# A recurrent layer's folds, operand copies and state store, shared out anew between ScalarE, VectorE and GpSimd

## The reference

```python
xw = jnp.einsum('ntd,dh->nth', x, Wx) + b
def step(prev_h, xw_t):
    next_h = jnp.tanh(prev_h @ Wh + xw_t)
    return (next_h, next_h)
_, hs = jax.lax.scan(step, h0, jnp.swapaxes(xw, 0, 1))
```

## Time and profile before

| | us |
|---|---|
| median of three runs | 7361.7 |
| profiled execution, its own time | 7363.88 |
| its span, first to last instruction | 7362.1 |
| of it the 128 steps of the recurrent layer, about | 3980 |

### The profile page before, as it was taken

How to read it: one execution, slowest core, us unless ns; L and a number is a source line. 1 busy time by engine, 2 the same in 40 slices (tenths; PEclk the granted TensorE clock), 3 DMA queues, 4 the chain that set the end, 5 groups by cost and what they waited for, 6 DMA issues and landing times. The chain is left out here.

```text
span 7362.1 us, 151269 instructions
## 1 busy us (share of the span) xinstructions
PE 5760.5 (78%) x49639; PEld 3129.6 (43%) x49913; DVE 5820.5 (79%) x11267; ACT 4421.0 (60%) x9397; POOL 2712.0 (37%) x2033
## 2 busy tenths in 40 slices
PE   5877787787778777877787707888888887943989
PEld 3555454455445555544454402333333333531543
DVE  4888988898889888988898669999999995455333
ACT  6877877787778777877787604444444442323322
POOL 2222222222222222222222108999999992000000
PEclk9999999999999999999999859999999998976989
DMA  0000000000000000000000010000000000000000
GB/s 7 2 2 2 2 2 2 2 2 2 2 2 2 2 2 2 2 2 2 2 2 2 10 34 5 4 4 4 4 4 4 4 4 3 0 10 3 0 17 6
DMA packets 14180, 30.30 MB, mean 4 GB/s; under 512 B 3665, under 2 KB 11602, under 8 KB 12434
## 3 DMA queue, kind: packets, MB, share of 16 engines
q1 hardware_dynamic: 13586, 22.47, 1.1%
HBM read 15.12 MB, written 7.34 MB: 3 GB/s over the span
## 5 line engine op out<-in xcount | busy, mean ns | idle before, releaser
L421 ACT ACTIVATE rx_junk<-rx_z 128x384 bf16<-128x384 f32 x2178 | 1371.9, 638 | 0.3
L1005 POOL TENSOR_TENSOR hc<-hh,cg 128x512 f32<-128x512 f32 x1024 | 1277.0, 1267 | 80.4 <-DVE hh L987 75.0
L927 ACT ACTIVATE ps_m<-ps_m,aneg 128x508 f32<-128x508 f32 x1024 | 673.6, 658 | 946.0 <-DVE hh L987 828.7
L987 DVE TENSOR_TENSOR_SCAN hh<-ps_m,bx 128x512 f32<-128x512 f32 x1024 | 1214.0, 1209 | 13.8 <-POOL bx L1009 13.8
L506 POOL TENSOR_TENSOR rx_z<-rx_z 128x512 f32<-128x512 f32 x256 | 384.9, 1504 | 2204.6 <-ACT rh_z L437 2201.5
L891 PE MATMUL ps_m<-hc,pick 128*128 128x512 f32 x2048 | 1056.3, 599 | 9.8 <-POOL hc L1005 8.5
L641 DVE TENSOR_REDUCE rh_ends<-rh_z 128x4 f32<-128x1536 f32 x512 | 960.3, 1919 | 131.0 <-ACT rh_z L437 131.0
L337 PE MATMUL r_ps<-rx_z,negid 128*128 128x256 f32 x2192 | 565.7, 405 | 280.2 <-POOL xsl L549 189.3
L512 POOL TENSOR_TENSOR rx_z<-rx_z 128x1024 f32<-128x1024 f32 x274 | 656.5, 2396 | 73.4 <-DVE rx_z L607 36.7
L313 PE MATMUL r_ps<-rh_z,negid 128*128 128x256 f32 x2048 | 496.8, 384 | 166.2 <-ACT r_ps L432 163.6
L337 PEld LDWEIGHTS r_ps<-rx_z,negid 128*128 128x128 f32 x2192 | 422.8, 202 | 391.0 <-issue 326.6
(11 more groups left out here) (397 smaller groups left out, 10726.0 us busy)
## 6 DMA issues: line engine op xcount, KB each, us to landing
rows_scratch<-pc SPq DMA_DIRECT2D x48, 128.0 KB
rows<-rows_scratch SPq DMA_DIRECT2D x128, 48.0 KB
ew<-in_e SPq DMA_DIRECT2D x3, 1024.0 KB, 7.0
rh_z<-in_x_dn SPq DMA_DIRECT2D x1, 1024.0 KB, 4.8
xcur<-in_x_dn SPq DMA_DIRECT2D x1, 1024.0 KB
out_x<-xcur SPq DMA_DIRECT2D x1, 1024.0 KB, 3.9
qi<-in_f_q SPq DMA_DIRECT2D x1, 384.0 KB, 2.9
xpw<-in_xp_t SPq DMA_DIRECT2D x1, 257.0 KB
```

What stands on the lines that cost most here:

```text
L421: e.activation(junk[:, n % JUNK], xz[i][:, :, n, 2:K2].rearrange("p c k -> p k c"), ACT.Copy, accum_out=xsum[:, i, n:n + 1]).then_inc(x_fo ...
L927: e.activation(da[un % NDA][:, :, 1:T], ps[:, un % 2, :].rearrange("p (n t) -> p n t", n=NG4)[:, :, 1:T], ACT.Exp, scale=aneg[:, 0:1]).the ...
L987: e.tensor_tensor_scan(hh[un % NBUF][:], da[un % NDA].rearrange("p n t -> p (n t)"), bx[un % NBUF][:], 0.0, ALU.mult, ALU.add).then_inc(sc ...
L1005: e.tensor_tensor(hc[un % NHC][:], hh[un % NBUF][:], cg[:], ALU.mult).then_inc(weighted, 1)
```

## The change

ScalarE folds the last two of the 16 sequences of the h chain (`TAIL = 2`), each with an ACTIVATE that accumulates into `ends`, behind its own last `rest` copy; VectorE's fourth reduction covers two sequences in place of four, and `pre` waits for `tail` as well. The four operand copies of the tanh move from ScalarE to GpSimd, as additions of zero or a subtraction from zero with two inputs each, behind the step's second `x_negdifference` and ahead of `x_bias`. The store of h moves from ScalarE to GpSimd, an addition of zero, behind `x_bias`; it waits for h itself, and the loads of `xsp` and `xsl` (s = 6 and 7) come after it in GpSimd's list. VectorE waits for the store of the step before (`kept`) ahead of the tanh.

```diff
@@ ScalarE, in a step
                     for c in range(2, NRC):
                         rest(c)
+                    e.wait_ge(ra, KA * t + A_REST[NRC - 1])
+                    for i_ in range(TAIL):
+                        n = N - TAIL + i_
+                        e.activation(rjunk[:, i_], hz[:, :, n, 2:K2].rearrange("p c k -> p k c"), ACT.Copy,
+                                     accum_out=ends[:, n:n + 1]).then_inc(tail, 1)
                     x_fold(g - 1, other, SECOND, THIRD)
-                    e.wait_ge(v, KV * t + V0 + VSQUARE)
-                    for lo, hi_ in ((1, 6), (7, 9)):
-                        e.activation(t0[:].rearrange("p (n j) c -> p n j c", j=GROUPS * GL)[:, :, lo:hi_, 0],
-                                     x2[:].unsqueeze(2).to_broadcast([128, N, hi_ - lo]), ACT.Copy).then_inc(tri, 1)
-                    e.wait_ge(v, KV * t + V0 + VGUESS)
...
-                    e.activation(entry(2), guess, ACT.Copy, scale=-1.0).then_inc(tri, 1)
-                    e.activation(entry(1), guess, ACT.Copy).then_inc(tri, 1)
                     x_fold(g - 1, other, THIRD, N)
...
-                    e.wait_ge(v, KV * t + V0 + KV)
-                    e.activation(hs[:, bass.ds(t, 1), :], h[:].unsqueeze(1), ACT.Copy).then_inc(ra, 1)
@@ GpSimd, in a step, behind the even sums and differences
+                    e.wait_ge(v, KV * t + V0 + VSQUARE)
+                    for lo, hi_ in ((1, 6), (7, 9)):
+                        wide = lambda x: x.unsqueeze(2).to_broadcast([128, N, hi_ - lo])
+                        e.tensor_tensor(t0[:].rearrange("p (n j) c -> p n j c", j=GROUPS * GL)[:, :, lo:hi_, 0],
+                                        wide(x2[:]), wide(nought[:]), ALU.add).then_inc(tri, 1)
+                    e.wait_ge(v, KV * t + V0 + VGUESS)
...
+                    e.tensor_tensor(entry(1), guess, none, ALU.add).then_inc(tri, 1)
+                    e.tensor_tensor(entry(2), none, guess, ALU.subtract).then_inc(tri, 1)
                     if s == 0:
                         e.wait_ge(xt_mm, i + 1)
                     x_bias(g - 1, s % 2, s)
+                    e.wait_ge(v, KV * t + V0 + KV)
+                    e.tensor_tensor(hs[:, bass.ds(t, 1), :], h[:].unsqueeze(1), nought[:].unsqueeze(1), ALU.add).then_inc(kept, 1)
                     if s == UN - 2:
                         e.wait_ge(xp_mm, UN * i + 2 * UN)
@@ VectorE, in a step
                     for c in range(NRC):
                         e.wait_ge(ra, KA * t + A_REST[c])
-                        j = tl.inc(e.tensor_reduce(ends[:, quarter(c)], fold(hz, quarter(c)), mybir.AxisListType.XY, ALU.add))
+                        n = slice(quarter(c).start, min(quarter(c).stop, N - TAIL))
+                        j = tl.inc(e.tensor_reduce(ends[:, n], fold(hz, n), mybir.AxisListType.XY, ALU.add))
                     tl.wait(j)
+                    e.wait_ge(tail, TAIL * t + TAIL)
...
                     j = tl.inc(e.tensor_tensor(pre[:], ends[:], xwT[:, s, :], ALU.add))
+                    e.wait_ge(kept, t + 1)
```

More of the change, by code:

```diff
@@ L79, in rnn @@
         ends = sb("rh_ends", [128, N])
+        TAIL = 2
+        rjunk = sb("rh_junk", [128, TAIL, D, 3], BF16)
         junk = sb("rx_junk", [128, JUNK, D, 3], BF16)
@@ L110, in rnn @@
             "x_copied", "x_summed", "x_evened", "x_negdiff", "x_rest", "x_folded", "x_biased"))
-        xt_mm, xw_cp, stp, stl, tri = (sem(x) for x in ("xt_mm", "xw_cp", "stp", "stl", "tri"))
+        xt_mm, xw_cp, stp, stl, kept, tri, tail = (sem(x) for x in ("xt_mm", "xw_cp", "stp", "stl", "kept", "tri", "tail"))
         KD = 8
@@ L117, in rnn @@
         A_REST = (7, 8, 11, 12)
-        KA = 13
+        KA = 12
         V_EVEN = (2, 5)
@@ L474, in _ @@
                         rest(c)
-                    x_fold(g - 1, other, SECOND, THIRD)
-                    e.wait_ge(v, KV * t + V0 + VSQUARE)
-                    for lo, hi_ in ((1, 6), (7, 9)):
-                        e.activation(t0[:].rearrange("p (n j) c -> p n j c", j=GROUPS * GL)[:, :, lo:hi_, 0],
-                                     x2[:].unsqueeze(2).to_broadcast([128, N, hi_ - lo]), ACT.Copy).then_inc(tri, 1)
-                    e.wait_ge(v, KV * t + V0 + VGUESS)
-                    guess = gs[:, 1:NS + 1].rearrange("p (ng j) -> p ng j", j=GL + 1)[:, :, 1:]
-                    entry = lambda c: t1[:, :, c].rearrange("p (ng j) -> p ng j", j=GL)
-                    e.activation(entry(2), guess, ACT.Copy, scale=-1.0).then_inc(tri, 1)
-                    e.activation(entry(1), guess, ACT.Copy).then_inc(tri, 1)
+                    e.wait_ge(ra, KA * t + A_REST[NRC - 1])
[3 more added lines that the diff above has]
+                                     accum_out=ends[:, n:n + 1]).then_inc(tail, 1)
+                    x_fold(g - 1, other, SECOND, THIRD)
                     x_fold(g - 1, other, THIRD, N)
@@ L492, in _ @@
                     x_fold(g, at, 0, FIRST)
-                    e.wait_ge(v, KV * t + V0 + KV)
-                    e.activation(hs[:, bass.ds(t, 1), :], h[:].unsqueeze(1), ACT.Copy).then_inc(ra, 1)
         @blk.gpsimd
         def _(e):
+            e.memset(gate[:, 2:3], 0.0).then_inc(kept, 1)
             e.memset(ident[:], 0.0).then_inc(setup, 1)
@@ L538, in _ @@
                         x_negdifference(g, (s + 1) % 2, c)
+                    e.wait_ge(v, KV * t + V0 + VSQUARE)
[4 more added lines that the diff above has]
+                    e.wait_ge(v, KV * t + V0 + VGUESS)
+                    guess = gs[:, 1:NS + 1].rearrange("p (ng j) -> p ng j", j=GL + 1)[:, :, 1:]
+                    entry = lambda c: t1[:, :, c].rearrange("p (ng j) -> p ng j", j=GL)
+                    none = nought[:, 0:1].unsqueeze(2).to_broadcast([128, N * GROUPS, GL])
+                    e.tensor_tensor(entry(1), guess, none, ALU.add).then_inc(tri, 1)
+                    e.tensor_tensor(entry(2), none, guess, ALU.subtract).then_inc(tri, 1)
                     if s == 0:
```

## The result

The changed kernel takes 7549.99 us in the median (7547.47 to 7551.38) against 7359.88 before: 1.0257 times as long, 95% interval 1.0239 to 1.0275, that is 190 us slower. Forecast were 7578 and a range of 7492 to 7690. The profiled execution took 7551.38, its span 7549.6; lines have moved by up to 12, so instructions are named by what they do.

A forecast was written before the change was run, and what follows sets the result against it. The x chain was taken to set the inner step, with the h chain some 0.2 us to spare. From the profiled 7363.9, 48 (inner steps) + 101 (step 6) + 67 (step 7) gave 7580, so 7578 against the median; range 7492 to 7690.

The forecast's parts named there:

- What bounds: Inner steps, ahead of `h_product`: the x chain sets the step; the h chain has some 0.2 us to spare.
- The fourth reduction: VectorE's reduction ahead of `pre`: halving saves between 0 and 0.94 us, but gain taken is 0.
- ScalarE's cover: Ahead of `x_rest_copy`: net some +0.7 us of work against 0.71 idle, taken as 0, bound ±0.2 per inner step.
- The copies and X: GpSimd's copies lengthen the tanh on the h chain by X = 0.75 us; inner steps grow by 0.5, +48 us.
- Step 6: Late `xsp` load +3.57, later h 0.75, slow clock 2.0: together 6.3 us in each of 16 blocks, +101 us.
- Step 7: Load of `xsl` delays `x_remainder`: +3.46 plus 0.75 for later h, 4.2 us in each of 16 blocks, +67 us.
- Copies in the gaps: Rival: GpSimd's copies find gaps in the tanh, inner steps stay at +0; 7507 us, chance 0.18.
- Whole-instruction exclusion: Rival: VectorE stands still throughout GpSimd's copies, 1.59 us with no time given back; 7688 us, chance 0.13.
- The loads not felt: Rival: TensorE's waits in steps 6 and 7 are covered by something else; between 7362 and 7426 us, chance 0.05.
- The h chain as bound with the saving getting through: Rival: h comes up to 0.96 us earlier in every step through `pre`; 7339 us, chance 0.02.

The follow-up runs named there:

- The folds alone: Kernel before with only ScalarE's two folds and the halved fourth reduction; copies and store stay on ScalarE: 7444.10 us, ratio 1.0114.
- halved warm matmuls: Kernel before with five warm matmuls in a step in place of ten: 7328.79 us, ratio 0.9955.
- the warm matmuls ahead of the wait: Changed kernel; in step 6 alone the ten warm matmuls stand ahead of TensorE's wait for `xsp`, not behind `product`: 7521.15 us, ratio 1.0222.
- the store alone: Kernel before with only the store of h moved to GpSimd, ahead of the loads: 7498.59 us, ratio 1.0189.
- the loads at the heads: Kernel before with the loads of `xsp` and `xsl` moved ahead of the even sums in steps 6 and 7: 7141.56 us, ratio 0.9708.

## Why the prediction was right, and where it was off

*What bounds.* Right: `h_product` stood behind the x chain and not behind h. The idle time ahead of it told that, and halving the warm matmuls showed it.

*The fourth reduction.* Right: 0.88 saved, none of it arrived. `pre` is held to 0.03 behind GpSimd's difference, and even without that the x chain would set the step. The folds alone cannot tell these two reasons apart; the rows of `pre` show the first, the halved warm matmuls the second.

*ScalarE's cover.* Right, and closer than could be claimed: `x_rest_copy` starts 5.86 behind the difference before and after, with 0.71 of idle time used up. With the four copies left on ScalarE the same start comes 0.62 late.

*The copies and X.* h moved from 8.82 to 9.50 behind the difference in the median inner step: X = 0.68, taken as 0.75. The four copies took 0.38, 0.29, 0.55 and 0.49, together 1.70 against the 1.59 of the line through 16 and 1024 elements. The two VectorE operations of 144 elements hold 0.46 of X. Off was what the h chain had to spare. It was read in one step, t = 45, as 0.24; in the halved-warm run the inner steps fell by 0.18 to 0.42, since in some steps the tanh has small delays of its own and t = 45 is one of the later ones. So the inner steps lost 28 us, not 48: the term that was most mis-sized. Some luck is in the 28: step 0 lost 0.52 in the median, and only 0.20 in the mean because low clock came with fewer turn ends than before (three of seven, before five). Why steps 0 and 1 lose about 0.5 and the others about 0.27 was not followed up.

*Step 6.* Right, 6.23 against 6.3, and part by part: the load was ready 1.26 behind h (forecast 1.4), h itself 0.63 later (0.75), and the clock cost about 2.1 (2.0). The lower end of that bound, no loss by the clock, falls with the warm matmuls ahead of the wait.

*Step 7.* Right in its mechanism, 3.98 against 4.2. Idle time for `xsl` went from 11.82 to 16.05 in the block shown, by the 4.2 that was forecast: the load was ready 1.26 behind h, but `x_remainder` followed it by 0.24 and not by 0.13. The missing 0.2 lies behind the idling, where the 16 matmuls took 5.13 in place of 5.50.

*The sum.* 48 + 101 + 67 = 216 was forecast, 190 came. The three parts of the change alone cost 27 (copies), 137 (store) and 83 (folds), 247 together; the whole costs less, since the removal of the copies from ScalarE pays for the folds: `x_rest_copy`, 0.62 late with the folds alone, is in time in the full change.

*The rivals.* Copies in the gaps (X near 0): refuted by the 23.0 us of waiting for VectorE. Whole-instruction exclusion, by which VectorE stands still throughout the copies: X was 0.68, not 1.59. How much of the difference is time given back, as with `pre` in the earlier trace rows, and how much is copies that ran in gaps was not separated. The loads not felt: refuted by the store alone. The h chain as bound with the saving getting through: refuted by the folds alone, where h comes no sooner, and by the halved warm matmuls, where the step falls though the h chain is untouched.

## What to carry to other kernels

Where two chains meet at one instruction, look at what that engine's idle time there names: if it never names the chain that is to be shortened, the saving is lost before it is made. An instruction that waits for a late value holds everything queued behind it on its engine; here a store of 0.22 us that nobody was waiting for cost 137 us, because a load stood behind it. And a load of a fixed operand belongs well ahead of its use, where its buffer is free and the engine idles: moving two loads gained 217 us, more than the change cost.

## What was not expected of the hardware

Of two engines that keep each other out, either one's row can hold the other's time: a one-element addition on GpSimd took 0.95 us beside a VectorE scan and 0.46 beside a diagonal of `pieces`, where 16 elements take 0.22 undisturbed, and `pre` took 1.18 us beside a difference. The duration of such an instruction is not its cost.

How long the clock stays low at a turn's end is not told by the idle time there. With the loads at the heads, idle times of 2.35 to 2.69 us came with 3.4 us of low clock (0.50, 1.2 of 2.4 GHz) at three of seven turn ends. In the changed kernel with the same move and in the one with half the warm matmuls besides, with 3.25 to 3.88 us of idling and a little more idle time in each step, it was 10 to 14 us at five and at four. But half the warm matmuls alone, with 3.59 to 4.08 us of idling, had 3.4 to 6.8 us at all seven. Why it takes the one or the other course was not settled by these runs.
